# Operands of the large matrix products moved to other places modulo 512 bytes

## The reference, cut to what matters

```python
x = x + _L0_attn_ref(_layernorm(x), in_proj_w, conv_w, conv_b, dt_bias, A_log, D, norm_w, out_w)
x = x + _L0_xattn_ref(_layernorm(x), ctx_1024, ctx_1024, 0, mask)
x = x + _L0_ffn_ref(_layernorm(x), A, B, Wr)
```

```python
proj = input_states @ in_proj_w.T                 # 2048 x 512 by 512 x 18560
gate, xBC, dt = split(proj)
xBC = silu(causal_conv4(xBC) + conv_b)
y = ssd(hs, A, Bm, Cm, D, dt, dt_bias)            # scan over time, per head
g = group_rms(y * silu(gate)) * norm_w
return g @ out_w.T                                # 2048 x 8192 by 8192 x 512
```

## Time and profile before

| | |
|---|---|
| median of 3 runs | 2847.12 us (2845.37 to 2847.9) |
| the profiled execution | 2843.42 us, span 2841.6 us |
| TensorE products | busy 2804.8 us (99%), 22298 instructions |
| weight loads | 2274.4 us (80%) |
| VectorE, ScalarE, GpSimd | 1990.1 (70%), 1462.6 (51%), 1315.5 us (46%) |
| chain that ended last | PE 91%, DVE 6%, ACT 1% |
| granted TensorE clock | 0.997 over the span |
| DMA | all from SyncE's queue, 578 MB, 61.5% of the 16 DMA engines' span |

### The profile page before, as it was taken

The page is one execution under the profiler, slowest core; times in us unless marked ns, Lnnn a source line. Parts: engine busy times, 40 slices in busy tenths (PEclk is TensorE's granted clock), DMA queues, the critical chain, the costliest instruction groups (busy, mean ns, idle before and its releaser), DMA issues.

```text
span 2841.6 us, 56494 instructions
## 1 busy us (share of the span) xinstructions
PE 2804.8 (99%) x22298; PEld 2274.4 (80%) x22298; DVE 1990.1 (70%) x3152; ACT 1462.6 (51%) x2205; POOL 1315.5 (46%) x840
## 2 busy tenths in 40 slices
PE   7999999999999999999999999999999999999998
PEld 5788888878788788887888888888888888878886
DVE  8777768887667757677676766677666666666767
ACT  5666656655445545445445454544545444453545
POOL 4766767775344333443343443424434334343334
PEclk9999999999999999999999999999999999999999
DMA  7788777778565555565665665555656656555530
GB/s 253 274 298 300 264 270 258 269 257 291 181 200 189 181 183 182 181 192 182 203 193 180 200 189 174 186 180 185 203 180 192 193 173 203 181 184 187 186 130 31
DMA packets 179428, 578.27 MB, mean 203 GB/s; under 512 B 25248, under 2 KB 31904, under 8 KB 171104
## 3 DMA queue, kind: packets, MB, share of 16 engines
q1 hardware_dynamic: 179168, 574.66, 61.5%
HBM read 460.29 MB, written 114.29 MB: 202 GB/s over the span
## 4 chain that ended last, share of the span: by engine, by line
PE 91%; DVE 6%; ACT 1%; issue 1%; DMA 0%; POOL 0%; SPq 0%; DVEq 0%; ACTq 0%; POOLq 0%
PE p_in L472 53%; PE p_out L472 23%; PE p_y L472 9%; PE p_in L562 4%; DVE cv L1430 1%; PE p_y L700 1%; DVE o_ring L1370 1%; DVE t_y L1479 0%; DVE g_f L1491 0%; DVE mx L1600 0%; ACT cv L942 0%; DVE sc L1587 0%; DVE cum L1392 0%; DMA raw_w<-wt 0%; DVE decay L1462 0%
## 5 line engine op out<-in xcount | busy, mean ns | idle before, releaser
L472 PE MATMUL p_in<-xnb,w_ring 128*128 128x512 f32 x6864 | 1673.2, 396 | 1.8 <-DVE cv L1430 0.9
L472 PEld LDWEIGHTS p_in<-xnb,w_ring 128*128 128x128 f32 x6864 | 1260.8, 188 | 262.6 <-issue 2.7
L1430 DVE SCALAR_TENSOR_TENSOR cv<-p_in,cpar,cv 128x504 f32<-128x504 f32 x954 | 699.8, 734 | 469.2 <-ACT cv L942 445.4
L1856 POOL TENSOR_TENSOR g_lo<-g_f,g_hi 128x512 fp32r<-128x512 f32 x256 | 338.1, 1322 | 1195.8 <-ACT g_hi L942 1195.8
L472 PE MATMUL p_out<-o_ring,g_hi 128*128 128x512 f32 x2048 | 638.3, 393 | 1.7 <-POOL g_lo L1856 1.7
L942 ACT ACTIVATE cv<-p_in,cpar 128x512 f32<-128x512 f32 x318 | 246.6, 775 | 636.9 <-PE p_in L472 600.5
L472 PEld LDWEIGHTS p_out<-o_ring,g_hi 128*128 128x128 f32 x2048 | 379.4, 188 | 80.3 <-issue 2.3
L472 PE MATMUL p_out<-o_ring,g_lo 128*128 128x512 f32 x1024 | 399.6, 390 | 0.0
L1467 DVE TENSOR_TENSOR x_tok<-p_in,dts 128x512 f32<-128x512 f32 x256 | 176.5, 689 | 285.7 <-PE p_in L562 284.0
L942 ACT ACTIVATE x_t<-cv 128x512 f32<-128x512 f32 x256 | 160.9, 628 | 309.9 <-DVE t_y L1479 285.9
L1867 POOL TENSOR_TENSOR ss<-ss,g_sq 128x512 f32<-128x512 f32 x190 | 310.3, 1633 | 7.4
(11 more groups left out here) (258 smaller groups left out, 2251.4 us busy)
## 6 DMA issues: line engine op xcount, KB each, us to landing
w_ring<-ws_scr SPq DMA_DIRECT2D x432, 512.0 KB, 3.7
o_ring<-ows_scr SPq DMA_DIRECT2D x192, 512.0 KB, 4.6
ws_scr<-w_ring SPq DMA_DIRECT2D x144, 512.0 KB, 5.9
decay<-cum_scr SPq DMA_DIRECT2D x126, 512.0 KB, 6.7
raw_w<-wt SPq DMA_DIRECT2D x144, 256.0 KB, 5.1
ows_scr<-o_ring SPq DMA_DIRECT2D x64, 512.0 KB, 6.3
raw_o<-owt SPq DMA_DIRECT2D x64, 256.5 KB, 5.6
acb<-x SPq DMA_DIRECT2D x3, 1024.0 KB, 7.7
```

What stands on the lines that cost most here:

```text
L472: return nc.tensor.matmul(o, lhsT=l, rhs=r, start=first, stop=last)
L1430: ins = V.scalar_tensor_tensor(acc[:, :, t:SEQ], src[:, :, 0:SEQ - t], cpar[:, 5 * m + 3 - t:5 * m + 4 - t], acc[:, :, t:SEQ], ALU.mult, A ...
L1856: T(g_lo[:, c % 2, :], g_f[:, c % 2, :], g_hi[:, c % 2, :].bitcast(F32), ALU.subtract).then_inc(glo_done, 1)
```

## The change

It alters where tiles lie, and nothing of what is computed or issued. `xnb0` now starts 32 bytes above a multiple of 512, `xnb1` 16 above one, `w_ring` stays at a multiple: the distance of a `unit` product is 32 in blocks 0 and 2 and 16 in blocks 1 and 3. `g_hi` and `g_lo` start 16 above a multiple of 512 and `o_ring` stays at one: the distance of a `project` product is -16, or 496 (the moving output weights lie 16 below the stationary gated rows). Three small tiles change places to fill the bytes (`ve`, `msv`, `rms`), and a tile `gap` of 496 bytes, which nobody uses, is new. The scratch area for DMAs that GpSimd would issue is halved to 8192 bytes a partition; the kernel issues none there. Everything behind it moves down by some 8 KB. `wd` now starts 384 above a multiple of 512, so the distance of `step_sizes` becomes 160 or 144. Tiles without an alignment of their own (`decay`, `x_tok`, `x_t`, `b_t`, `c_t` and others) start 64 above a multiple of 512 instead of at one.

On each of the five engines the instructions of the changed kernel are the same as before and in the same order; only the addresses differ.

```diff
-        msv = sb("msv", [P, QT])
-        rms = sb("rms", [P, QT])
         st6 = sb("st6", [P, QT, 6])
         mv = sb("mv", [P, QT, 2])
-        ve = sb("ve", [P, QT])
+        rms = sb("rms", [P, QT])
...
-        xnb = [sb(f"xnb{b}", [P, 2, KT, TB], F32R, align=2048) for b in range(2)]
+        ve = sb("ve", [P, QT])
+        xnb = [sb("xnb0", [P, 2, KT, TB], F32R, align=32)]
+        gap = sb("gap", [P, 124], align=16)
+        xnb.append(sb("xnb1", [P, 2, KT, TB], F32R, align=16))
...
         o_ring = sb("o_ring", [P, RING_O, 2, HID], F32R, align=2048)
-        g_hi = sb("g_hi", [P, 2, TB], F32R, align=2048)
-        g_lo = sb("g_lo", [P, 2, TB], F32R, align=2048)
+        msv = sb("msv", [P, QT], align=16)
+        g_hi = sb("g_hi", [P, 2, TB], F32R, align=16)
+        g_lo = sb("g_lo", [P, 2, TB], F32R, align=16)
...
-    nc = bacc.Bacc("TRN2", target_bir_lowering=False, num_devices=1)
+    nc = bacc.Bacc("TRN2", target_bir_lowering=False, num_devices=1, dynamic_dma_scratch_size=8192)
```

## The result

| | before | changed |
|---|---|---|
| median | 2846.24 us of 4 runs (2842.27 to 2847.9) | 2877.38 us of 4 (2875.84 to 2879.39) |
| ratio | | 1.0113, 95% interval 1.0100 to 1.0125 |
| profiled execution, span | 2843.42, 2841.6 us | 2875.84, 2874.1 us |

The change made the kernel 1.1% slower, 31 us. The prediction said 56 us faster, in a range up to 2893 us: the time lies in the range, on the wrong side of before.

What follows compares the result with a forecast made beforehand. The prediction took TensorE's product periods to bound the kernel. One term of -56 us, the others 0, took the profiled 2843.42 us to 2787, or 2791 us for the median; the 8-in-10 range was 2740 to 2893 us.

Steps and rivals of the forecast that it cites:

- What bounds the kernel: Whole kernel: TensorE, 99% busy, hardly waits; only the products' period, 226.6 ns against 213.3 for the columns, can give time.
- Step 1: All engines: no instruction is added, dropped or moved, so no wait is added; cost 0.
- step 2: Other engines' writes of `xnb`, `g_hi` and `g_lo` at new starts: taken as 0, far end 33 us.
- Step 4: Small products of `step_sizes`, distance 192 to 160 and 144: at most 1 us, taken as 0.
- Step 3: Large unit and output products at distances 32, 16, -16: period falls by up to 6.7 ns, -56 us taken.
- Rival A: All `unit` and `project` products: distance costs as at 192, +67 us, +46 units only, +23 one block's kind; chance 0.33.
- Rival B: Large products: distance doesn't matter, `wd` is slower for its own reason; time stays 2847 us, give or take 5; chance 0.14.
- C: Large products: the collision goes altogether, period 213.3 to 217 ns, -96 to -133 us; chance 0.08.
- What would show it: Large products' median durations: near 382 ns if right, wrong if 389 or more; blocks 1, 3 against 0, 2 tell distances.

Runs made afterwards that it cites:

- The map: Bare probe without the kernel's computation: 48-product runs at 256 pairs (moving, stationary operand's bytes above a multiple of 512); none under 226.7 ns, mean 231.6.
- nine pairs: Bare probe, computation left out: nine operand places each, float32r and bfloat16, several widths; 512 columns at (0, 0) took 226.7 ns, bfloat16 215.8 at all nine.
- 11 entries: Bare probe, computation left out: twelve pairs, each entered behind one product of 256 to 328 columns or 24 products at (0, 0); (0, 16) took 226.7 or 233.3 ns.

## Why the prediction was wrong

*What bounds the kernel* was right. All of the 31 us are TensorE's periods: 6333 x (232.34 - 228.51) = 24.3 us in the units and 2749 x (232.51 - 227.27) = 14.4 us in the output, 38.7 in all; the other periods of TensorE, first products and short ones, are 6 us shorter in sum (span +32.5). Much of these 6 us may be the clock: the mean granted to the profiled executions was 0.9967 before and 0.9984 in the changed kernel, with TensorE busy for 12.0 and 3.9 us at the lower level, which at half speed is worth some 4 us, an estimate.

*Step 1* (no wait added, cost 0) and *step 2* (writers of misaligned tiles, 0) held: the busy time of ACT and POOL rose by 4.7 and 3.6 us, 0.3%, and the wait for `g_lo` fell to 0.9 us. *Step 4* can't be told from 0: the products by `wd` average 397 ns in both.

*Step 3 is the step that failed, by its sign.* I had bounded the period between 213.3 and 233.3 ns and took the measured 6.7 ns as a gain, because I thought that an offset of 16 or 32 bytes would part two readers who start on the same spot. The only row of another distance, the products by `wd` at 233.3 ns, said the opposite, and I set it aside with a picture for which no row spoke. The map gives what stands in its place: 231.7 ns at 16, 233.3 at 32, 233.3 at 192, and 226.7 at 0, the lowest of 256 pairs. Where the sum has -56 us for this step, the periods of the large products added 38.7. The line-by-line collision that I read into the 32 lost columns is not shown by these runs either; a pair that parts the readers altogether doesn't exist in the map.

*Rival A* was what happened, with the place it named. Its price was off by a factor of two (67 us against 31), for four reasons. It counted all 9984 products, where 9082 have such a period (6 us). It started from 226.6 ns, while the periods before average 228.5 in the units, since more than a third of them are not in the short cycle (14 us with the output). It put all at 233.3, where the changed kernel has 232.3 and 232.5 (8 us). And it left out the 6 us by which the rest became shorter. By kinds it said 46 us for the units alone, measured 27; the output alone costs nothing, which no case of mine had. Its mechanism, that every place but 0 is like the row of `wd`, is not right as it stands: 80 bytes over a stationary operand at 16 is as short as 0.

*Rival B*, with the Trainium skill's rule of independent ports for the two operands ("TensorE: Matmul & The Clock Gate", "Step-by-step: what each phase is for"), falls: with nothing but TensorE at work the same form takes 11.15 or 11.45 us by its places. In bfloat16 the nine pairs tried are equal (215.8 ns), so for that type the rule agrees with the runs. For float32r, where the distance between the two operands changes the period by up to 10 ns, it doesn't. *C* falls with the map.

*What would show it*: the medians did, 396 and 394 ns. Blocks 1 and 3 against 0 and 2 told 16 from 32 as foreseen: 231.6 against 233.1 and 233.0 ns, some 1580 x 1.4 = 2.2 us a block.

Left open: why the cycles are what they are. Many of the steady periods found are multiples of 6.67 ns (120.0, 173.3, 226.7, 233.3, 240.0), which a fixed beat of that length would give, but no run isolates it. Whether the loss goes when no weights are loaded beside the stream, and which read of the weights meets which read of the moving operand, was not tried.

## What to carry to other kernels

A trace with one slow and one fast row of the same instruction is a measurement of the thing in which they differ; take its sign as well as its size, and don't overrule it with a mechanism that no row shows. Where TensorE streams float32r back to back, the places of both operands are a tuning knob worth up to 6% of a product (226.7 to 241.7 ns): put both at multiples of 32 bytes at equal places modulo 256, or better at a pair that comes to the short period from every entry, and measure pairs in a bare loop entered in several ways, since one entry can flatter a pair: (32, 16) is as good as any in the map and had the longer cycle in 5 of 11 entries. A part of a change that costs nothing alone can cost beside the rest, because the slow cycle is handed on from one group of products to the next.

## What the runs showed of the hardware that was not expected

- The period of float32r products depends on the places of both operands, 226.7 to 236.7 ns in steps of 16 bytes, up to 241.7 in steps of 4, with a distance modulo 256 and, for most pairs, a stationary place modulo 32; that of bfloat16 products did not change over nine pairs (215.8 ns).
- At (0, 0) the loss over the columns is per product and not per column: 13.3 ns at 512, 384 and 256 columns.
- A pair can have two steady periods: (0, 16) gave 226.7 ns in 4 of 11 entries and 233.3 in 7.
- The way into the short cycle takes 3 to 10 products at (0, 0) behind a short product (the very first run left out), and 0 to 6 at (80, 16). With the units moved there, the kernel is 0.26% faster.
